# Sliding-window attention and a ternary feed-forward: where the transposed scores stand in PE's slot

## The reference

```
x = x + layernorm(attention(layernorm(x)))
x = x + layernorm(feedforward(layernorm(x)))

attention:    q, k, v = x @ Wq.T + bq, ...        16 heads of 32
              each block of 256 queries sees its own 256 keys and the 256 before,
              of these the last 256 up to the query itself
              softmax(q k / sqrt(32)) v, then @ Wo.T + bo
feedforward:  h = x @ T1.T + gate * (x @ v.T @ fast_b.T @ u.T)     hidden 2048, rank 16
              r = max(h, 0);  (r * r) @ T2.T
```

## Time and profile before

| what | value |
|---|---|
| median of 3 runs | 2378.9 us (2378.79 to 2380.89) |
| the profiled execution's own time | 2378.28 us |
| its span, first to last instruction | 2376.6 us |
| mean granted TensorE clock | 0.976 of full |
| PE busy | 2217.4 us, 93% of the span |
| DVE, ACT, POOL busy | 71%, 69%, 57% |
| DMA | 159.90 MB, mean 67 GB/s |

### The profile page before, as it was taken

The page is one execution under the profiler, slowest core; times in us unless marked ns, Lnnn a source line. Parts: engine busy times, 40 slices in busy tenths (PEclk is TensorE's granted clock), DMA queues, the critical chain, the costliest instruction groups (busy, mean ns, idle before and its releaser), DMA issues.

```text
span 2376.6 us, 60643 instructions
## 1 busy us (share of the span) xinstructions
PE 2217.4 (93%) x20124; PEld 1645.5 (69%) x20124; DVE 1696.3 (71%) x4247; ACT 1643.4 (69%) x4613; POOL 1355.0 (57%) x2473
## 2 busy tenths in 40 slices
PE   3267899999999999999999999999999999999998
PEld 2244677777777777777777777777777777777665
DVE  7535677777777777777777777777777777777754
ACT  4326777677767777677766777677776777677762
POOL 2023566566656666666665666665665666655553
PEclk9588999999999999999999999999999999999999
DMA  6112223322223222222222232232222322232210
GB/s 224 27 44 69 59 62 72 76 70 61 63 69 72 60 68 73 73 62 71 60 66 69 66 74 63 71 71 62 63 64 74 73 70 60 73 67 53 59 30 27
DMA packets 323336, 159.90 MB, mean 67 GB/s; under 512 B 203456, under 2 KB 293568, under 8 KB 322512
## 3 DMA queue, kind: packets, MB, share of 16 engines
q1 hardware_dynamic: 323024, 156.03, 26.7%
HBM read 46.83 MB, written 16.78 MB: 27 GB/s over the span
## 4 chain that ended last, share of the span: by engine, by line
PE 82%; SPq 5%; DMA 3%; ACT 2%; DVE 2%; issue 1%; POOL 0%; POOLq 0%; ACTq 0%; DVEq 0%
PE Ab L781 19%; PE F L836 19%; PE F L863 15%; PE Cb L781 9%; PE Ob L771 7%; PE Tb L754 6%; PE S L740 5%; SPq L691 5%; PE F L848 3%; DMA x2T<-xs 2%; DMA xT<-xs 1%; ACT PT L924 1%; ACT Sm L910 0%; DVE lnst L1044 0%; DVE Sm L1027 0%
## 5 line engine op out<-in xcount | busy, mean ns | idle before, releaser
L924 ACT ACTIVATE PT<-Tb 128x384 f32<-128x384 f32 x896 | 438.8, 490 | 418.9 <-PE Tb L754 413.7
L910 ACT ACTIVATE Sm<-Sm,nmax 128x384 f32<-128x384 f32 (+2 forms) x1024 | 584.2, 571 | 129.7 <-DVE nmax L1027 126.1
L1027 DVE CUSTOM_DVE_ANT_0 Sm<-S,mask,scales 128x384 f32<-128x384 f32 (+2 forms) x1024 | 572.2, 563 | 120.6 <-PE S L740 109.9
L836 PE MATMUL F<-x2T,t 128*128 128x256 f16 x4096 | 489.1, 272 | 0.0
L863 PE MATMUL F<-t,r 128*128 128x512 f16 x2048 | 483.5, 379 | 0.7 <-DVE r L1129 0.7
L836 PEld LDWEIGHTS F<-x2T,t 128*128 128x128 f16 x4096 | 397.9, 98 | 52.2
L781 PE MATMUL Ab<-xT,w_attn 128*128 128x256 f16 x3072 | 384.5, 276 | 37.0 <-DMA xT<-xs 32.3
L781 PEld LDWEIGHTS Ab<-xT,w_attn 128*128 128x128 f16 x3072 | 294.0, 99 | 95.5 <-issue 49.3
L1239 POOL TENSOR_SCALAR_AFFINE_SELECT PT<-PT 128x256 f32<-128x256 f32 x512 | 260.8, 513 | 173.5 <-ACT PT L924 172.7
L863 PEld LDWEIGHTS F<-t,r 128*128 128x128 f16 x2048 | 195.5, 98 | 201.0 <-ACT r L974 4.6
L740 PE MATMUL S<-QK 96*128 96x384 f16 (+2 forms) x1280 | 315.4, 280 | 10.3 <-DVE nmax L1027 10.3
(11 more groups left out here) (158 smaller groups left out, 3007.7 us busy)
## 6 DMA issues: line engine op xcount, KB each, us to landing
QK<-qkp SPq DMA_DIRECT2D x1536, 32.0 KB, 1.9
xa<-in_x SPq DMA_DIRECT2D x64, 256.0 KB, 2.9
x<-in_x SPq DMA_DIRECT2D x64, 256.0 KB, 3.0
out<-yc SPq DMA_DIRECT2D x64, 256.0 KB, 2.2
stage<-in_w_fc SPq DMA_DIRECT2D x4, 1024.0 KB, 9.2
stage<-in_w_proj SPq DMA_DIRECT2D x4, 1024.0 KB, 5.8
turned<-parts SPq DMA_TRANSPOSE x128, 2.3
stage<-in_Wq SPq DMA_DIRECT2D x1, 1024.0 KB, 5.5
```

Source lines behind the costliest of these rows:

```text
L836: pe.matmul(Fb[b][:, half * STEP:(half + 1) * STEP], W["t1"][:, k, mc * P:(mc + 1) * P], x2T[:, part, k, :], start=(half == 0 and k == 0 a ...
L910: act.activation(blk, blk, ACT.Exp, bias=nmax[:, hg % 2, j % 8:j % 8 + 1], scale=-1.0, accum_out=sums[:, hg % 2, j % 8:j % 8 + 1]).then_in ...
L924: act.activation(PT[:, n % NPT].rearrange("p b n -> p (b n)"), Tb[:, 0:WIN], ACT.Exp, bias=1.0, scale=c_score).then_inc(M["T_exp"], 1)
L1027: v.tensor_tensor_reduce(Sm[:, j % NSM, c0:WIN], Sb[j % 2][:, c0:WIN], W["mask"][:, c0:WIN], W["c"][:, 3:4], 3e38, ALU.add, ALU.min, nmax[ ...
```

## The change

In PE's body the call of `scores_transposed` stands directly behind `scores`, ahead of `weighted_values` and of all products, and no longer at the end of the slot. Nothing else is changed; tables, lags, buffers and semaphores are as before, and so are the programs of the other four engines.

```
                 for s in range(SLOTS):
                     if it.has(0):
                         scores(it.t, it.p, s)
+                    ok, t, p, i = lagged(it, s, LAG_T)
+                    if ok and tile_of(p, i):
+                        scores_transposed(t, p, i)
                     ok, t, p, i = lagged(it, s, LAG_PV)
                     if ok and i % GROUP == GROUP - 1 and tile_of(p, i):
                         weighted_values(t, p, i // 8, i // GROUP % 2)
...
                     for t, p, (i, piece) in due(it, FF2_SLOT, s, 0, -1):
                         ff_out(t, i, piece)
-                    ok, t, p, i = lagged(it, s, LAG_T)
-                    if ok and tile_of(p, i):
-                        scores_transposed(t, p, i)
```

## The result

The changed kernel takes 2394.18 us (median of 4 runs, 2392.98 to 2396.39) against 2378.85 (2376.69 to 2380.89): a ratio of 1.0066, 95% interval 1.0048 to 1.0083. The forecast was 2382 with a range of 2371 to 2408 and 0.42 for slower.

A forecast was written before the change was run, and what follows sets the result against it. The prediction took PE, a closed stream of matmuls with 13.2 us idle, as the bound; 9.6 + 1 us of added waits less 4.2 and 3 removed gave +3.4 on 2378.9, about 2382 us, range 2371 to 2408.

The forecast's parts named there:

- forecast A: Whole kernel: advance and tighter deadline nearly cancel, 2376 to 2388 us, taken at 2382; chance 0.43.
- B: Slots 23 to 30: PE waits for Tb's read-out because DVE holds ACT's list back; 2403, up to 2433 us; chance 0.32.
- the sum: Whole kernel: waits added less waits taken away, 9.6 + 1 - 4.2 - 3 = +3.4 us.
- PE is a closed stream; only waits count: PE, steps 2 to 31: 13.2 us idle; T's 0.17 us costs the same anywhere, so sum 0.
- ACT's and SP's advance: Earlier T lets ACT's list run 1.15 us earlier (slot 20, step 14) and SP's stack about 2 us earlier.
- the 150 named: Sign of being right: ACT's wait for the transposed scores falls from 382.6 us to under 150.
- Slot 23, 0.3 us x 24: T 1.1 us late for the exponential freeing Tb; DVE's advance leaves 0.2 to 0.6, taken as 0.3 in 24 steps.
- Slot 28, 0.1 us x 24: T 1.15 us late for DVE's shift copy; DVE's advance leaves 0 to 0.2, taken as 0.1 in 24 steps.
- I went through the places of a step: Check of where ACT's or DVE's work comes late against the scores; it named slots 23, 28, 30 and 2.
- Slot 2: T 1.7 us late behind the x2T transfer, which starts about 2 us earlier: 0 left; otherwise 41 us.
- Gains of 7.2 us: Old PE waits taken away: 4.2 us of the projection product for ACT, about 3 us for L924.
- The clock: Rival: waits of a few tenths in each slot could bring PE to its lower clock; over 2450 us, chance 0.02.

The follow-up runs named there:

- e9_slot27: Kernel before, with T earlier in slot 27 alone, behind the weighted values and ahead of the product; 2369.40 us, ratio 0.9965.
- e1_place: Changed kernel, with DVE's copy of the shift one slot earlier (lag 4, not 5); 2384.48 us, ratio 1.0025 to the kernel before.
- e8_residual: Changed kernel, with POOL's first residual one slot later in POOL's list (lag 2, not 1); 2406.64 us, ratio 1.0118 to the kernel before.
- e2_ahi: Changed kernel, with ACT's split of a row block moved from slot 16 to 17, DVE's and SP's parts following; 2384.64 us, ratio 1.0028 to the kernel before.
- e7_before_stack35: Kernel before, with the stack of head group 1 moved from slot 29 to slot 35 in SP's queue; 2650.75 us, ratio 1.1144.

## Why the prediction was right or wrong

The direction that it held likeliest, slower (0.42 against 0.38 for no change), and the time within its range were right. The point was 12 us low, and the time lies outside the forecast A's own 2376 to 2388, between A and the 2403 of B, where no rival stands. So the direction is in part luck: the sum said +3.4 us, less than a measurement can tell from nothing, and what made the kernel slower is one place that is not in the sum and one that stands there at a quarter of its size.

- **PE is a closed stream; only waits count.** Right. T's columns cost the same in either place, and the loss in steps 3 to 30 is the difference of the waits, to within 1 us. That the waits view before holds them all was wrong: 4 us of tenths at slots 18 and 25 were hidden in modelled durations.
- **ACT's and SP's advance.** Right. The wait of ACT for T fell to 142 us, under the 150 named; the stack moved by 2.2 us against the scores (e9_slot27 shows that this release alone takes away the waits of slots 2 and 3; those of slots 18 and 25 it leaves).
- **Slot 23, 0.3 us x 24.** It was 0.1 us, 2.4 in all. The chain was read rightly and over-priced.
- **Slot 28, 0.1 us x 24.** Mis-sized: 10.6 us in 28 steps. The copy did advance 0.8 us against the scores, but stayed at 1.22 us, and I had counted on a further 0.2 to 0.5 from waits paid ahead of it. The copy stayed long beside the residual, as the prediction had said it would by the shared interface. e1_place and e8_residual show start and length as the causes.
- **Slot 17.** The step that failed: "I went through the places of a step" left it out, and it is the largest term, 13.3 us. Its lateness in the trace of before, 1.4 us, stood there as plainly as slot 23's. The prediction gives no reason for leaving it out; ACT would have had to come forward by 1.4 us. It won 0.9, and e2_ahi shows that its own list of slot 16 holds it. In the changed kernel L1129 beside POOL takes 1.53 us at slot 14 (it took 0.68), and its mean over the kernel rose from 737 to 837 ns (60 of them now begin while POOL's square runs, 1 before); that this took part of the advance is argued, not shown.
- **Slot 2.** Half right: 1.5 us earlier, not 2, and that leaves 0.35 us in the second steps.
- **Gains of 7.2 us.** In steps 3 to 30 about 12 were gained, with 2.8 more ahead of step 3, where I had counted at most 2.
- **The clock.** Its price, over 2450, did not come: the clock reads 1.00 from step 2 to 31 in the changed kernel. But the reading behind it, that a short wait costs its own length because the long stretch reads 1.00, was wrong. The wait of 4.0 us is followed by at least 3 us at 0.50, and in e7_before_stack35 each wait of 7 us costs more than its length too. The waits in step 2 of the changed kernel, 1.2 us at most, left the clock at 1.00.

Sum by the same terms, measured: +31.0 of waits at T, -13.2 of old waits, -2.8 and +0.8 at the ends, 15.8 in all, against +10.6 - 7.2.

Rival B's mechanism (ACT's gain ends at DVE) is there in the 344.7 us that ACT now waits for masked scores, but not its places: of the 1.1 us a step that PE waits at T, half a microsecond is at slot 17, which is ACT's own list, and 0.1 at slot 23. Two signs of being wrong that the prediction named are met: more than 1 us of waits a step at T, and a wait at a slot not named with ACT's own list as its cause, by which the slack was read wrongly.

## What to carry to other kernels

When an operation is moved earlier on a full engine, list for every slot of the period how late its releaser would be in the old trace, and let none drop out by judgment: three places of 0.1 to 0.5 us, 24 to 28 times, decide such a change. Look for which of its waiters profits and how much lead it needs; here one release in 32 slots gave 9.6 us, but 4.3 of them in a single step, and half of the move gave 15 where the whole lost 15. And look where in the run a gain lies before it is put down to the loop: here one wait of 4 us, with the lower clock behind it, was nearly half of it.

## What the runs showed of the hardware that was not expected

DVE's copy of the shift or L1129, begun while one of POOL's larger operations runs, ends a fixed time past POOL's end, the copy 0.29 us and L1129 0.55: the copy takes 0.42 alone and 1.22 beside the residual, L1129 0.68 alone and up to 1.74. Begun first, they keep their length. In e8_residual, moving the POOL operation moved the loss to the next DVE operation. T restarts 0.06 us after ACT's read of the bank ends, so the round trip through one bank costs hardly more than ACT's 0.49 us.

PE went on at half the clock after standing 4.0 us in step 2 (0.50 from 261.0 to 264.0 us) and after each wait of 7 us in e7_before_stack35, where a product of 1.48 us then took 2.77.
